# Adapter-and-FFN kernel: four base blocks transposed ahead of the pairs instead of five, the fifth by VectorE, and loads and gathers put in another order

## The reference, cut to what matters

```
# x: 32 sequences x 64 tokens x 1024, adapter_ids: one of 16 per sequence
w = weight[adapter_ids]                       # 1024 x 1024 for each sequence
c = einsum('bsi,boi->bso', x, w)              # layer 0, first product
logits = c @ W_router.T                       # 8 experts, top 2, softmax weights
h   = einsum('td,erd->ter', c, lora_A)        # rank 16
l0  = c @ W_base.T + b_base + 2 * einsum('ter,eor,te->to', h, lora_B, w_top2)
x   = x + l0
# layer 1: one of 16 64x64 mixes per sequence, columns permuted, 16 heads of
# 64 -> 256 -> 64 with gelu, columns permuted back
y = einsum('bct,bcd->bdt', x, weights[adapter_ids])
x = x + unperm(down(gelu(up(y[:, perm]))))
```

## Time and profile before

| | |
|---|---|
| median of three runs | 613.79 us |
| the profiled execution, its own time | 612.9 us |
| its span | 611.1 us |
| TensorE busy | 97% of the span |
| VectorE busy | 77% |
| ScalarE, GpSimd busy | 24%, 21% |
| mean HBM traffic | 174 GB/s over the span, 300 to 410 GB/s up to 245 us |
| granted TensorE clock | full in every slice |

### The profile page before, as it was taken

The page is one execution under the profiler, slowest core; times in us unless marked ns, Lnnn a source line. Parts: engine busy times, 40 slices in busy tenths (PEclk is TensorE's granted clock), DMA queues, the critical chain, the costliest instruction groups (busy, mean ns, idle before and its releaser), DMA issues.

```text
span 611.1 us, 13485 instructions
## 1 busy us (share of the span) xinstructions
PE 592.6 (97%) x4375; PEld 348.2 (57%) x4376; DVE 471.5 (77%) x1303; ACT 144.6 (24%) x290; POOL 127.1 (21%) x194
## 2 busy tenths in 40 slices
PE   4999999999998999999999999999999999999996
PEld 3344444344433444457777676767676767676762
DVE  3068778878887779698888897779987889887862
ACT  2100000200020002153332524225332235232334
POOL 4010002121111220060022222222231313131312
PEclk9999999999999999999999999999999999999999
DMA  7999889899899997120023222222222222222222
GB/s 269 409 388 316 306 307 305 308 308 315 297 409 403 352 316 254 44 69 28 19 63 94 70 90 68 88 73 88 70 86 69 88 67 94 69 86 67 88 71 86
DMA packets 43428, 106.90 MB, mean 175 GB/s; under 512 B 8451, under 2 KB 17667, under 8 KB 43395
## 3 DMA queue, kind: packets, MB, share of 16 engines
q1 hardware_dynamic: 30914, 76.04, 35.7%
q0 software_dynamic: 6784, 21.51, 10.6%
q10 hardware_dynamic: 5696, 8.95, 4.2%
HBM read 98.09 MB, written 8.39 MB: 174 GB/s over the span
## 4 chain that ended last, share of the span: by engine, by line
PE 86%; DVE 6%; DMA 4%; issue 2%; ACTq 0%; SPq 0%; POOL 0%; DVEq 0%; another core or an unknown queue 0%; POOLq 0%
PE wide L536 26%; PE bank L643 20%; PE bank L651 10%; PE bank L731 8%; PE wide L714 8%; PE y_wide L567 4%; DVE c_pair L1096 3%; DMA ring<-adapters_dram 3%; PE y_wide L689 3%; PE wide L551 2%; DMA x_in<-x_seq_dram 1%; PE bank L663 1%; PE bank L664 1%; PE bank L667 1%; PE bank L743 1%
## 5 line engine op out<-in xcount | busy, mean ns | idle before, releaser
L536 PE MATMUL wide<-ring,x_in 128*64 128x512 f32 x960 | 209.6, 592 | 2.4 <-DMA ring<-adapters_dram 2.4
L536 PEld LDWEIGHTS wide<-ring,x_in 128*64 128x64 f32 x960 | 73.1, 137 | 127.1 <-issue 127.1
L1288 DVE STREAM_TRANSPOSE x_tok<-xres 32x128 f32<-32x128 f32 x464 | 140.2, 302 | 6.0
L1096 DVE STREAM_TRANSPOSE c_pair<-wide 32x256 f32<-32x256 f32 x240 | 107.1, 446 | 39.4 <-issue 21.7
L943 ACT ACTIVATE act_sb<-wide 128x512 f32<-128x512 f32 x120 | 66.5, 610 | 191.3 <-PE wide L714 191.3
L643 PE MATMUL bank<-c_hi,base_t 128*128 128x512 f32 x384 | 102.3, 390 | 0.0
L424 POOL DMA_INDIRECT xres<-xT_dram,row_in x32 | 35.0, 1094 | 230.8 <-DVE out_sb L1278 227.6
L643 PEld LDWEIGHTS bank<-c_hi,base_t 128*128 128x128 f32 x384 | 71.9, 188 | 15.3
L651 PE MATMUL bank<-c_lo,base_t 128*128 (+1 forms) x256 | 78.0, 390 | 0.0
L462 POOL COPY c_all<-c_pair 128x512 f32 x30 | 19.3, 669 | 213.9 <-DVE c_pair L1096 213.9
L858 ACT ACTIVATE small<-small 128x1 f32<-128x1 f32 x16 | 3.2, 203 | 217.3 <-DVE small L1132 217.3
(11 more groups left out here) (161 smaller groups left out, 601.5 us busy)
## 6 DMA issues: line engine op xcount, KB each, us to landing
ring<-adapters_dram SPq DMA_DIRECT2D x128, 512.0 KB, 5.8
x_in<-x_seq_dram ACTq DMA_DIRECT2D x32, 256.0 KB, 4.8
down_sb<-down_dram SPq DMA_DIRECT2D x32, 128.0 KB
up_raw<-up_dram SPq DMA_DIRECT2D x62, 64.0 KB
ar_sb<-lora_a_router_dram ACTq DMA_DIRECT2D x1, 544.0 KB, 4.3
mix_sb<-mix_dram SPq DMA_DIRECT2D x32, 16.0 KB, 2.0
xres<-xT_dram,row_in POOLq DMA_INDIRECT x32, 3.5
out_dram<-out_sb,row_out POOLq DMA_INDIRECT x28, 3.0
```

Of the source, the lines that this page charges most:

```text
L536: last = pe.matmul(acc[half][h][z * TOK:(z + 1) * TOK, :], x_in[:, half, z, k, :], ring[:, k, z, h * HALF:(h + 1) * HALF], start=(k == 0), ...
L1096: last = nc.vector.transpose(c_pair[r * SQ:(r + 1) * SQ, :, q * SQ:(q + 1) * SQ], wide[half][q * SQ:(q + 1) * SQ, :, :] .rearrange("p h (k ...
L1288: last = nc.vector.transpose(x1_tok[q * SQ:(q + 1) * SQ, :].rearrange("p (c f) -> p c f", f=P)[:, :, f * SQ:(f + 1) * SQ], xres[f * SQ:(f ...
```

## The change

`SOON` goes from 5 to 4 and a name `LOOPED` = 3 takes the place of `KT - SOON`, so the loops keep their three rounds and blocks 5 to 7. Block 4 is gathered by GpSimd into `raw_tile` once pair 0's x has landed, turned by VectorE in 16 transposes before `turn_pair(0)` and copied by ScalarE after the x issues of pair 1. `stay_busy` has 4 transposes instead of 8. SP issues slots 2 to 7 of pair 0 only once pair 0's x has landed. ScalarE does a copy of one column before the wait for `lists_ok`. `turn_four` is done in two parts: 4 of its 16 transposes after the route of the pair before, 12 in their old place. The 16 gathers of `b_rows` and `bias` stand in t = 10 to 13, four in each, instead of t = 4 to 11, two in each.

```diff
-SOON = 5
-BUSY = 8
+SOON = 4
+LOOPED = KT - SOON - 1
+BUSY = 4
-GATHERS = range(PAIRS // 4, PAIRS // 4 + KT)
+GATHERS = {PAIRS - 6 + n: (2 * n, 2 * n + 1) for n in range(KT // 2)}
@@ first_pair (SP)
                 for k in range(KT):
+                    if k == 2:
+                        sp.wait_ge(x_in_in[0], 32)
                     sp.dma_start(ring[:, k, 0, :], adapters[bass.ds(first, 1), k * P:(k + 1) * P, :]
@@ gpsimd
+            pool.wait_ge(x_in_in[0], 32)
+            on_its_own()
+            gather(raw_tile[:, :], w_base, perm_sb[:, SOON:SOON + 1], tile_in)
             pool.wait_ge(order_ok, 1)
             for t in range(PAIRS - 1):
                 keep_pair(t)
-                if t % 4 == 0 and t // 4 < KT - SOON:
-                    j = t // 4 + SOON
-                    if t > 0:
-                        pool.wait_ge(tile_turned, t // 4)
+                if t % 4 == 0 and t // 4 < LOOPED:
+                    j = t // 4 + SOON + 1
+                    pool.wait_ge(tile_turned, t // 4 + 1)
                     gather(raw_tile[:, :], w_base, perm_sb[:, j:j + 1], tile_in)
-                if t in GATHERS:
-                    j = t - GATHERS[0]
+                for j in GATHERS.get(t, ()):
                     gather(b_rows[:, j, :], lora_b, perm_sb[:, j:j + 1], b_in)
                     gather(bias[:, j:j + 1], bias_rows, perm_sb[:, j:j + 1], bias_in)
@@ scalar
             act.sem_inc(hw_placed, 8)
+            act.wait_ge(ident_ok, 2)
+            nc.scalar.copy(th, ident[:, 0:1])
             act.wait_ge(lists_ok, 1)
             load_x(0, 0)
             for j in range(SOON):
                 base_copied(j)
             load_x(1, 1)
+            tile_kept(-1)
@@ vector
-            def turn_four(i):
-                dve.wait_ge(hw_ok, i * 4 + 4)
-                dve.wait_ge(hw_placed, i * 8 + 8)
-                for q in range(P // SQ):
+            def turn_four(i, qs):
+                if qs[0] == 0:
+                    dve.wait_ge(hw_ok, i * 4 + 4)
+                    dve.wait_ge(hw_placed, i * 8 + 8)
+                for q in qs:
@@
+            turn_tile(-1, range(0, 16))
             turn_pair(0, 0)
             route(0)
-            with dve.Fori(0, KT - SOON) as i:
+            with dve.Fori(0, LOOPED) as i:
@@
                     else:
-                        turn_four(i)
+                        turn_four(i, range(1, 4))
                     route(t, hw_four[:, (n + 1) % 4, :])
+                    if n == 2:
+                        turn_four(i, range(0, 1))
```

More of the change, by code:

```diff
@@ L883, in tile_kept @@
             def tile_kept(i):
-                act.wait_ge(tile_turned, i + 1)
-                nc.scalar.copy(base_rows[:, bass.ds(i + SOON, 1), :, :].rearrange("p a k o -> p (a k o)"), c_tok[:, :]) \
+                act.wait_ge(tile_turned, i + 2)
+                nc.scalar.copy(base_rows[:, bass.ds(i + SOON + 1, 1), :, :].rearrange("p a k o -> p (a k o)"), c_tok[:, :]) \
                     .then_inc(base_turned, 1)
@@ L906, in _ @@
                 tanh(half)
-            with act.Fori(0, KT - SOON) as i:
+            with act.Fori(0, LOOPED) as i:
                 for n in range(4):
@@ L1174, in turn_tile @@
                 if pieces[0] == 0:
-                    dve.wait_ge(tile_in, (i + 1) * 16)
-                    dve.wait_ge(base_turned, i + SOON)
+                    dve.wait_ge(tile_in, (i + 2) * 16)
+                    dve.wait_ge(base_turned, i + SOON + 1)
                 for n in pieces:
@@ L1193, in turn_four @@
                                                    hw_four[r * SQ:(r + 1) * SQ, :, q * SQ:(q + 1) * SQ])
-                last.then_inc(hw_turned_ok, 1)
+                if qs[-1] == P // SQ - 1:
+                    last.then_inc(hw_turned_ok, 1)
             def pair(t, half):
```

## The result

The changed kernel takes 615.5 us (median of 18 runs, 612.53 to 617.57), the kernel before 612.39 (18 runs, 611.07 to 614.24). The ratio on record is 1.0042, with a 95% interval of 1.0032 to 1.0053: slower by 2.6 us (the two medians lie 3.1 apart; this text goes by the ratios). The forecast was faster by 2.3 us, with a range that ended at 615.3. It was counted from 613.79, the median of three runs of the kernel before, which lies 1.4 above that of the 18. The profiled execution after took 614.87 us with a span of 613.1; that of before had a span of 611.1. So the traces have 2.0 us between them.

The account below looks back on a forecast made before the run. TensorE, busy for 97% of the span, was taken as the bound, so only its standstills pay. Start -1.6, turn_four -0.5 and gathers -0.2 gave -2.3 us, 613.8 to 611.5; range 609.2 to 615.3 with rival 1 and rival 3.

Parts of the forecast that it names:

- x: Pair 0's x lands 4.8 us after issue instead of 7.40, so pair 0 starts at 15.5, 2.6 us sooner.
- The start: Up to pair 0: x's gain of 2.6 us less a ring stall of 1.0, in sum -1.6 us.
- turn_four: Four of 16 transposes moved ahead into idle time remove the router's wait: -0.5 us.
- rival 1: Ring starves pair 0, or x lands as late as before; the sum is 0, 613.8 us; chance 0.20.
- the rule beside the sum: DMA engines take turns between queues, so the number of busy queues slows x, not depth; x lands near 7.4 us.
- The ring: Slots 2 to 7, issued after x, stall pair 0 between 0 and 2.3 us, taken as 1.0.
- Block 4: Its transposes move to VectorE's idle stretch, 7.0 us, done at 28.8 to 30.7; cost 0.
- cover: Slack of 1.1 us between the end of turn_pair(0) and the router's start, so block 4 costs 0.
- The gathers in the full stretch: Two pairs of gathers leave 173 to 191 us, where the DMA engines are full: -0.2 us (0 to -0.5).
- The gathers in t = 10 to 13: Four gathers in a row; the copy of h_l slips into the second gap at about its old time: 0.
- Rival 2: Gathers form a wall: h_l waits until 0.6 us after the fourth gather, 9.2 us added, 620.7; chance 0.11.
- rival 3: The copy of h_l goes in the third gap, 0.9 us late each time, 3.6 in all: 615.1 us; chance 0.08.

Follow-up runs that it names:

- a1: The changed kernel with the gathers of b_rows and bias back in t = 4 to 11, two in each; 613.84 us, ratio 1.0022.
- a2: The kernel before with only the gathers of b_rows and bias moved, four in each of t = 10 to 13; 612.52 us, ratio 1.0002.
- b2: The kernel before with only turn_four split in two parts; 612.45 us, ratio 1.0007.
- s1: The changed kernel with the gathers behind route(t) and without SP's wait, the whole ring queued beside x; 612.19 us, ratio 0.9997.
- p1: The changed kernel with ScalarE also waiting for the router's semaphore before each tanh, then copying one column; 616.86 us, one run.
- a3: The changed kernel with two tiny VectorE operations between the wait for the router and the copy of h_l; 614.16 us, one run.
- a4: The changed kernel with the same four gathers in t = 10 to 13 held until route(t) ends; 612.80 us, ratio 1.0003.
- m1: The changed kernel with plain loads of the same size, unpermuted, in place of the gathers of b_rows and bias; 611.80 us, ratio 0.9991.
- p2: The changed kernel with the bias gathers one each in t = 2 to 9, only two b_rows gathers in each of t = 10 to 13; 612.34 us, one run.
- b1: The kernel before, start unchanged, with turn_four in two parts and four gathers behind route(t) in t = 10 to 13; 611.74 us, ratio 0.9989.
- c1: b1 (start of the kernel before) with the table load taken early; 611.22 us, ratio 0.9981.
- e2: a4 with 24 idle transposes instead of 4 ahead of pair 0; 611.84 us, ratio 0.9991.
- e1: s1 with 24 idle transposes instead of 4 ahead of pair 0; 612.82 us, ratio 1.0007.
- s2: a4 with SP's wait for x moved ahead of slot 0, so no ring slot is queued beside x; 614.91 us, one run.

## Why the prediction was wrong

**x.** This is the first term that failed, and the larger: 4.8 us from issue to landing, measured 7.15. The start was put at -1.6 us and came to +0.9 in the trace; start and `turn_four` together were put at -2.1, and a1, which has both and not the move of the gathers, has +1.3. Pair 0 started 0.8 us sooner instead of 2.6, of which 0.5 are x's earlier issue (10.13 instead of 10.67) and the rest its landing. Even the 0.5 isn't clearly the change's: a2 and b2, with the old start, issue x at 10.25 and 10.14, s1 and p1, with the new one, at 10.65 and 10.66. I took the median of all landings, most of which lie in the pairs, where other queues have little to do. The landing that stood in the same place, 7.40, was the one to take. It is the case named at the end of rival 1, x as late as before, and the rule beside the sum had said so.

**The ring.** The stall of 1.0 us was right in kind (1.44 in the profiled execution after; 1.6 to 3.2 in a3, a4 and p1, and none in a1, m1 and p2, whose clock fell). But it was set against a gain that didn't come. What was missing is a second price: TensorE is ready at 14.4, as predicted (14.5), and stands still for 3.0 us. After such a gap the clock fell in a1, m1 and p2, which costs 15.4 or 15.65 - 13.95 = 1.5 to 1.7 us. The prediction put nothing for it. The start came to +0.9 us in the trace. By ratios it costs 1.0003 - 0.9989 = 0.0014, 0.9 us, between a4 and b1, and 0.0022, 1.3 us, between a4 and c1. The intervals overlap in the first pair and touch in the second. e2 suggests that filling the gap gives back about as much (0.9991 against a4's 1.0003, intervals that overlap).

**Block 4.** The cost was 0 as predicted, with a smaller cover. After, VectorE in order of time, the line that answers to the earlier trace rows:

```profile
26.30 7.18 DVE L1186 STREAM_TRANSPOSE c_tok<-raw_tile 32x256 f32<-32x256 f32 x16 [15.59 <-DMA raw_tile<-w_base_dram,perm_sb]
33.51 7.34 DVE L1103 STREAM_TRANSPOSE c_pair<-wide 32x256 f32<-32x256 f32 x16
```

The gather landed 8.1 us after its issue, the longest that I had allowed, and after a later issue (18.08 instead of 15.5). The transposes ended at 33.48, not 30.7, and pair 0 was over at 33.0. (The prediction says 7.0 us for the transposes and reckons with 7.2; they took 7.18.) The router began at 41.42 without a wait, because pair 0's stall had moved it too. Without that stall the same edit costs 0.7 us in s1 and 1.7 in e1.

**turn_four.** The 0.5 us came, but for another reason. I gave them to the split; b2 keeps the wait, a1 has it again, and a2, without the split, is free of it. The move of the gathers took it away: a hit by luck.

**The gathers in the full stretch.** The ring waits around pair 10 went from 2.4 to 1.1 us, more than the 0.2 predicted. But b2, with the gathers in their old place, has 1.2, and a4, with them gone, has 2.1 in three. These waits vary by over a microsecond between executions, and no gain can be read from them.

**The gathers in t = 10 to 13.** This is the second term that failed: priced at 0, the new place costs 2.9 us between t = 10 and the end of the pair stage in the trace. By ratios it costs 1.2 us against the old place in the changed kernel (after less a1) and 0.1 in the kernel before (a2); against a place behind the route it costs 2.4 (a4). The premise was wrong. I took what the rows show (a copy 0.6 us after a gather, one in a gap) for a copy that slips into gaps. But the copy of t = 5 has no idle time before it in the earlier trace rows: VectorE came to it from other work at 121.71, and the router was over 0.4 us after the first gather's start, where the signal was never seen late. That row shows no gap letting anything through. It is TensorE's signal that is late, and the gaps of 0.3 us don't reliably let it through: 0.6 us after the second gather in t = 11, at the end of the third in t = 10, 1.1 us after the fourth in t = 13. Rival 2 had the right consequence on TensorE's side, but held the copy to be what waits, and its sum of 9.2 us assumed the worst in each of four pairs. Measured are 2.3, 1.9 and 4.5 us in t = 10, 11 and 13, of which VectorE's slack left TensorE waits of 0.2, 1.2 and 1.1 us. That rival 3's figure, 615.1, comes close to 615.5 is luck: its terms are others, and it was counted from 613.8 where the kernel before has 612.39.

The parts don't add up. By ratios a1 has 1.3 us and a2 0.1, in sum 1.4, and the whole has 2.6. a2's profiled execution (614.47 us) is its slowest and shows the full wall, while its median is 612.52. How late the signal comes varies with where the router's end meets the gathers, as the traces show. That a2's faster executions are those in which the routers end early in the row is argued and not shown, and why the wall costs less with the old start stays open.

## What to carry to other kernels

A row of indirect loads on GpSimd should not stand where another engine waits for TensorE: put it behind the route that needs the signal (one wait on GpSimd; 2.4 us in the changed kernel, 0.8 with the old start, a2 against b1, with intervals that overlap). A copy that has no idle time before it tells nothing of the signal it waited for. A transfer is priced by the landing that stood beside the same busy queues; holding back the depth of another queue bought some tenths of a microsecond at most here. An edit that makes TensorE ready sooner for something that isn't sooner creates a gap, and the gap has a price of its own, the clock behind it (about 1.6 us where it fell).

## What the runs showed of the hardware

- TensorE's semaphore signal reached VectorE and ScalarE at the same instant, up to 4.7 us late, while GpSimd executed a row of indirect loads (p1), and 0.2 us behind the router beside four plain loads of the same bytes (m1). Where the router was over 0.8 us or more after the first gather's start, the signal came 1.1 to 1.7 us behind it with two gathers (before, a1, b2, p2) and 1.2 to 4.95 with four (after, a2, a3, p1).
- A lone indirect load delayed the signal until 0.4 us after its own end where the router was over 0.55 to 0.87 us after its start (after, a1, m1, p2), and not at all where that was 0.4 us (a3, s1, e1).
- Two 256 KB halves of x landed in 3.19 us with the ring's queue idle (s2), in 6.62 to 7.39 with two slots of 512 KB on it (eight executions), and in 7.12 and 7.50 with eight (s1, e1).
- The granted clock fell from 1.00 to 0.50 (1.2 GHz) after TensorE had stood still for 1.95 us (b1, e2), 2.56 (m1), 2.63 (a1), 3.41 (p2) and 4.68 (s2), and stayed at 1.00 after 2.17 (c1), 2.38 (a4), 2.77 (p1), 2.93 (s1), 2.96 (after) and 3.21 (a3). So the length of the gap alone doesn't tell. Where it fell just ahead of pair 0 (a1, m1, p2, s2), that pair took 15.4 to 16.8 us instead of 13.95.
